# A feed-forward norm taken by halves, one copy of the feed-forward for either kind of weights, and a new order of calls on four engines

## What is computed

```python
# layer 0
h = layernorm(x) * (1 + ca) + sa
x = x + ga * attention(h)        # 16 heads of 16, causal, norm of q and k
h = layernorm(x) * (1 + cb) + sb
x = x + gb * ffn(h)              # silu(h W1) * (h W2), gelu(. H1), gelu(. H2), . W3
# layer 1
h = layernorm(x) * (1 + ca) + sa
x = x + ga * scan(h)             # in-projection, 16-state selective scan over time, gate, out-projection
h = layernorm(x) * (1 + cb) + sb
x = x + gb * (mx_quantize(h) @ mx_quantize(w).T + bias)
```

## Time and profile before

| | |
|---|---|
| median of 3 runs | 4168.96 us (4165.49 to 4177.01) |
| profiled execution | 4167.61 us |
| its span, first to last instruction | 4165.8 us |
| busy | TensorE 85%, VectorE 80%, GpSimd 65%, ScalarE 62% |
| granted TensorE clock, mean | 0.932 of full speed |
| instructions | 50421 |
| read from and written to HBM | 212.25 and 31.46 MB |

### The profile page before, as it was taken

How to read it: one execution, slowest core, us unless ns; L and a number is a source line. 1 busy time by engine, 2 the same in 40 slices (tenths; PEclk the granted TensorE clock), 3 DMA queues, 4 the chain that set the end, 5 groups by cost and what they waited for, 6 DMA issues and landing times. The chain is left out here.

```text
span 4165.8 us, 50421 instructions
## 1 busy us (share of the span) xinstructions
PE 3523.9 (85%) x16621; PEld 2034.0 (49%) x16621; DVE 3318.2 (80%) x3646; ACT 2583.4 (62%) x3703; POOL 2716.0 (65%) x1960
## 2 busy tenths in 40 slices
PE   5687888989899998989898898989999898989513
PEld 3263645546373645546373554636364554636201
DVE  4514878989798888979797887979898897979694
ACT  2345566767667676766666676767667676666431
POOL 0132866768595876768595776759586776768563
PEclk9799999999999999999999999999999999999756
DMA  4630201102030301103030211203030211203000
GB/s 164 258 105 15 97 21 62 62 26 97 6 117 1 97 26 61 62 21 102 6 102 17 82 41 46 77 8 115 1 107 16 76 46 41 82 6 102 0 5 5
DMA packets 69435, 247.81 MB, mean 59 GB/s; under 512 B 9472, under 2 KB 10112, under 8 KB 68736
## 3 DMA queue, kind: packets, MB, share of 16 engines
q1 hardware_dynamic: 66816, 235.35, 16.8%
q10 hardware_dynamic: 2304, 8.39, 0.5%
HBM read 212.25 MB, written 31.46 MB: 59 GB/s over the span
## 5 line engine op out<-in xcount | busy, mean ns | idle before, releaser
L671 POOL TENSOR_TENSOR kept<-kept,hb 128x512 f32<-128x512 f32 x640 | 811.0, 1300 | 71.1 <-DVE hb L1925 70.9
L1916 DVE TENSOR_TENSOR_SCAN hb<-ps,hb 128x512 f32<-128x512 f32 x640 | 745.0, 1205 | 17.5 <-ACT ps L1362 12.7
L929 PE MATMUL ps<-hid_bhi,wring 128*128 128x512 f32 x1536 | 628.0, 409 | 70.9 <-issue 53.6
L929 PE MATMUL ps<-hid_blo,wring 128*128 128x512 f32 x1536 | 619.8, 404 | 0.0
L1362 ACT ACTIVATE ps<-kept,a_neg 128x512 f32<-128x512 f32 x640 | 423.0, 690 | 174.4 <-DVE hb L1916 174.4
L929 PE MATMUL ps<-hid_ahi,wring 128*128 128x512 f32 x1280 | 516.7, 404 | 8.0 <-POOL hid_alo L686 8.0
L639 POOL TENSOR_TENSOR kept<-kept,hb 128x1024 f32<-128x1024 f32 x128 | 300.2, 2360 | 336.3 <-DVE hb L1860 297.7
L929 PE MATMUL ps<-hid_alo,wring 128*128 128x512 f32 x1280 | 505.0, 395 | 0.0
L632 POOL TENSOR_SCALAR_AFFINE_SELECT room<-room 128x512 f32<-128x512 f32 x256 | 217.7, 862 | 427.2 <-ACT room L1569 427.2
L1988 DVE TENSOR_REDUCE room<-ps 128x4 f32<-128x2048 f32 (+3 forms) x256 | 375.2, 1486 | 123.6 <-PE ps L1105 111.3
L1925 DVE TENSOR_TENSOR hb<-hb,ps 128x512 f32<-128x512 f32 x640 | 404.0, 673 | 0.1
(11 more groups left out here) (198 smaller groups left out, 7359.2 us busy)
## 6 DMA issues: line engine op xcount, KB each, us to landing
wring<-w_hi SPq DMA_DIRECT2D x352, 512.0 KB, 3.3
kept<-in_wffn SPq DMA_DIRECT2D x22, 512.0 KB, 6.3
w_hi<-wring SPq DMA_DIRECT2D x22, 512.0 KB, 7.0
w_lo<-wrest SPq DMA_DIRECT2D x22, 512.0 KB, 5.2
xn<-in_x_fm SPq DMA_DIRECT2D x17, 512.0 KB, 3.3
out_fm<-xc ACTq DMA_DIRECT2D x16, 512.0 KB, 5.4
room<-in_wmod SPq DMA_DIRECT2D x2, 1536.0 KB, 8.1
win<-in_win SPq DMA_DIRECT2D x1, 1024.0 KB, 8.4
```

The costliest lines, as they stand in the source:

```text
L671: pool.tensor_tensor(acc[:, m, :], acc[:, m, :], hb[:, s % 8, :], ALU.add).then_inc(acc_done, 1)
L929: mm = pe.matmul(bank(bk), wring[:, r % 3, at + k * P:at + (k + 1) * P], src[i][:, k, :], start=(k == 0 and i == 0), stop=(k == K - 1 and ...
L1916: dve.tensor_tensor_scan(hb[:, s % 8, :], bank(2 + m % 2), hb[:, s % 8, :], 0.0, ALU.mult, ALU.add).then_inc(scanned, 1)
```

## The change

1. The feed-forward's norm has semaphores of its own and goes by halves: mean, centring, square, variance and scaling are two calls each. The affine calls are now `ffn_round(c)` and `ffn_full(c)`, in the order round 0, full 0, round 1, full 1. `att_proj` goes by output half.
2. The first two products of the feed-forward are split: `up_high(1)` and `up_high(0)` need only the rounded halves of h, `up_low(0)` and `up_low(1)` the rests.
3. The weights' rest is no longer stored. The first pass subtracts in place in the stage buffer and measures it, and the buffer is reloaded only after that. If there is a rest, the whole weights are loaded as they are and multiplied in plain float32, in a second copy of the feed-forward. The flag is asked for once in a pass, by TensorE and by SyncE.
4. The order of calls on TensorE, ScalarE, VectorE and GpSimd is new.

The diff, cut to its core:

```diff
-        wrest = sb("wrest", [P, 2, HM * P], F32R)
+        wraw = sb("wraw", [P, 2, HM * P])
 def split_sync(sp):
-            for t in range(FT + 2):
+            for t in range(FT + 1):
                 if t < FT:
                     if t >= 3:
-                        sp.wait_ge(w_split, t - 2)
+                        sp.wait_ge(w_measured, t - 2)
                     sp.dma_start(stage[:, t % 3, :], a["wffn"][t]).then_inc(stage_loaded[t % 3], 16)
...
-                    sp.wait_ge(w_split, r + 1)
-                    sp.dma_start(w_lo[r], wrest[:, r % 2, :].bitcast(F32)).then_inc(lo_stored[r % 2], 16)
...
-                dve.tensor_tensor(wrest[:, t % 2, :], stage[:, t % 3, :], wring[:, t % 3, :].bitcast(F32), ALU.subtract).then_inc(w_split, 1)
+                dve.tensor_tensor(stage[:, t % 3, :], stage[:, t % 3, :], wring[:, t % 3, :].bitcast(F32), ALU.subtract).then_inc(w_split, 1)
 # TensorE: norm, first products, choice
+            def ffn_mean(c):
+                    pe.wait_ge(att_added, since(att_added, c + 1 if att else DC))
+                    mm = pe.matmul(bank(4), mean_mat[:, :], xa[:, c, :], start=(c == 0), stop=(c == DC - 1))
+            def ffn_var(c):
+                    pe.wait_ge(f_cent, since(f_cent, DC))
+                    pe.wait_ge(f_sq, since(f_sq, c + 1))
+                    mm = pe.matmul(bank(4), mean_mat[:, :], ln_s[:, c, :], start=(c == 0), stop=(c == DC - 1))
+            def up_high(n, exact):
+                    pe.wait_ge(h_rounded, since(h_rounded, DC))
+                    wait_tile(0, exact)
+                    if n == 0:
+                        ... tail_y, head_y
+                    else:
+                        ... ff_added, dt_min
+                    up_product(n, 0, exact)
+            def up_low(n, exact):
+                    pe.wait_ge(h_split, since(h_split, DC))
+                    up_product(n, 1, exact).then_inc(up_done, 1)
+                with pe.If(has_rest > 0):
+                    feed_forward(False)
+                with pe.Else():
+                    feed_forward(True)
 # TensorE's order around the norm
-            head_spread(1, 1)
-            att_proj(0)
-            values(3, 0) values(3, 1) values(3, 2) row_sums(3)
-            att_proj(1) att_proj(2) att_proj(3)
-            fin_back(0) fin_back(1)
-            ffn_mean() spread(0, 2) ffn_var() fin_ff(0) spread(1, 2) fin_ff(1)
-            up(0) up(1) up(2) spread(0, 3) up(3) ...
+            fin_back(0) head_spread(1, 1)
+            att_proj(0, 0) att_proj(1, 0) values(3, 0) att_proj(0, 1) att_proj(1, 1)
+            values(3, 1) values(3, 2) row_sums(3)
+            att_proj(2, 1) att_proj(2, 0) att_proj(3, 0) att_proj(3, 1)
+            ffn_mean(0) ffn_mean(1) spread(0, 2) fin_back(1) ffn_var(0) ffn_var(1) fin_ff(0) fin_ff(1)
+            up_high(1) spread(1, 2) up_high(0) up_low(0) up_low(1) up(2) spread(0, 3) up(3) ...
 # TensorE's order in the attention stage (one example)
-            scores(3, 0) out_proj(1) scores_turned(2, 0) fin_mean() head_spread(1, 0) scores(3, 1) values(1, 2)
-            fin_var() scores_turned(2, 1) row_sums(1) scores(3, 2)
+            scores(3, 0) out_proj(1) head_spread(1, 0) scores_turned(2, 0) fin_mean() scores(3, 1)
+            fin_var() scores_turned(2, 1) values(1, 1) values(1, 2) scores(3, 2)
 # VectorE
+            tail_in(3, 0) tail_scan(3, 0) tail_out(3, 0) tail_scan(3, 1) tail_out(3, 1)
-            ffn_scale() times_b(2, 0) ff_add(0) scan(2, 0) times_b(2, 1) ff_add(1) times_c(2, 0) gate_up(0)
+            ffn_scale(0) ffn_scale(1) ff_add(0) ff_add(1) times_b(2, 0) scan(2, 0) times_c(2, 0) gate_up(0)
...
-            scan(11, 0) times_c(11, 0) next_scale() scan(11, 1) ffn_add(1) times_c(11, 1)
+            scan(11, 0) next_scale() times_c(11, 0) times_b(11, 1) ffn_add(0) ffn_add(1) scan(11, 1) times_c(11, 1)
 # GpSimd
-            causal_probs(2, 2) causal_probs(3, 0) quant_at(0, 12) causal_probs(3, 1) quant_at(1, 3) causal_probs(3, 2)
+            causal_probs(2, 2) quant_at(0, 3) quant_at(0, 12) causal_probs(3, 0) causal_probs(3, 1) causal_probs(3, 2) quant_at(1, 3)
 # SyncE, once in a pass
-                for r in range(3, FT):
-                    ... load w_hi[r]
-                    with sp.If(has_rest > 0):
-                        ... load w_lo[r]
+                with sp.If(has_rest > 0):
+                    ... load a["wffn"][r], r = 0 to 21, into wraw
+                with sp.Else():
+                    ... load w_hi[r], r = 3 to 21
```

More of the change, by code:

```diff
@@ L838, in pre_var @@
                 if pre:
[L839 removed]
+                    pe.wait_ge(f_norm, since(f_norm, 0))
                     if att:
@@ L912, in next_var, with wait_tile, product @@
                     mm.then_inc(next_var_done, 1)
-            def product(bk, r, at, src, K, fresh=None):
-                for k in range(K):
-                    if k == K - 1:
-                        with pe.If(has_rest > 0):
-                            pe.wait_ge(rest_loaded[r % 2], since(rest_loaded[r % 2], 16 * (r // 2 + 1)))
-                            for i in range(K):
-                                if fresh is not None:
-                                    pe.wait_ge(hid_split, since(hid_split, fresh + i + 1))
-                                for part_of in src:
-                                    pe.matmul(bank(bk), wrest[:, r % 2, at + i * P:at + (i + 1) * P], part_of[:, i, :],
-                                              start=False, stop=False)
+            def wait_tile(r, exact):
+                if exact:
+                    pe.wait_ge(w_loaded[r % 3], since(w_loaded[r % 3], 16 * (r // 3 + 1)))
+                else:
+                    pe.wait_ge(raw_loaded[r % 2], since(raw_loaded[r % 2], 16 * (r // 2 + 1)))
+            def product(bk, r, at, src, K, exact, fresh=None):
+                for k in range(K):
                     if fresh is not None:
@@ L1160, in att_proj @@
                     pe.wait_ge(o_normed, since(o_normed, quad + 1))
-                    for m in range(DC):
-                        mm = pe.matmul(bank(m), wu[:, quad, m * P:(m + 1) * P], o_sb[:, quad, :], start=(quad == 0), stop=(quad == QUADS - 1))
-                        if quad == QUADS - 1:
-                            mm.then_inc(att_out, 1)
+                    mm = pe.matmul(bank(m), wu[:, quad, m * P:(m + 1) * P], o_sb[:, quad, :], start=(quad == 0), stop=(quad == QUADS - 1))
+                    if quad == QUADS - 1:
+                        mm.then_inc(att_out, 1)
             project(0)
@@ L1309, in tensor_pass, with feed_forward @@
-            spread(1, 11)
-            mid(17)
+            def feed_forward(exact):
+                up_high(1, exact)
+                spread(1, 2)
+                up_high(0, exact)
+                up_low(0, exact)
+                up_low(1, exact)
+                up(2, exact)
+                spread(0, 3)
+                up(3, exact)
+                up(4, exact)
+                up(5, exact)
+                up(6, exact)
+                up(7, exact)
+                spread(1, 3)
+                spread(0, 4)
+                mid(0, exact)
+                mid(1, exact)
+                spread(0, 5)
+                spread(1, 4)
+                mid(2, exact)
+                mid(3, exact)
+                mid(4, exact)
+                spread(0, 6)
+                spread(1, 5)
+                mid(5, exact)
+                mid(6, exact)
+                spread(0, 7)
+                spread(1, 6)
+                mid(7, exact)
+                mid(8, exact)
+                spread(1, 7)
+                spread(0, 8)
+                mid(9, exact)
+                mid(10, exact)
+                spread(0, 9)
+                spread(1, 8)
+                mid(11, exact)
+                mid(12, exact)
+                mid(13, exact)
+                spread(0, 10)
+                spread(1, 9)
+                mid(14, exact)
+                mid(15, exact)
+                spread(0, 11)
+                next_mean()
+                spread(1, 10)
+                mid(16, exact)
+                next_var()
+                spread(1, 11)
+                mid(17, exact)
```

510 lines of the change are left out of this document (247 added, 263 removed).

## The result

The changed kernel took 4176.12 us, median of 12 runs (4168.27 to 4185.08), beside 4165.84 for the kernel before on the same chips (4163.98 to 4177.01). The ratio is 1.0021, with a 95% interval of 1.0014 to 1.0029: a hair slower, and inside the 0.3% that I called no change. I had forecast 4074. The profiled execution took 4173.6 us (span 4171.9).

What follows compares the result with a forecast made beforehand. TensorE, VectorE and GpSimd fill the third stage; TensorE idles 20.4 us a pass in the first two. 14 x (-4.5 - 1) = -77, the rest -18, together -95: 4167.6 to 4072.6, plus 1.4 for the median: 4074; range 4015 to 4140.

Steps and rivals of the forecast that it cites:

- The norm: Ahead of the feed-forward: halves and early high products bring the first gate 4.6 us sooner; -4.5 us a pass, bounds -3, -6.
- The stretch behind the gate: Feed-forward beside the scan's body: TensorE keeps its lead, every spread is met, the tightest with 1.3 us to spare.
- The order in the first stage: Loop's attention stage: TensorE's new order moves work into waits; -1 us a pass, bounds -5 and +3.
- my walk: Call-by-call estimate of the attention stage's new order: its projection ends at 1605.0 for 1605.4.
- a first stage longer than 129 us: Named sign of being wrong: the loop's attention stage, 126.3 us before, takes over 129 us.
- My slower case: After the far jump TensorE fetches each following packet only when it reaches it: 4224 us; chance 0.06.
- The first pass: Weights' split without the stored rest: 1.0 MB a tile for 1.5, 60 us for 90; -12 us, between -17 and -3.
- under 80: Sign to look for in the first pass: the split's stretch, 90 us before, should take under 80.
- The jump: TensorE's one jump a pass over the second feed-forward copy: cost 0, at most 3.3 us; rival exposed, 4124 us, chance 0.14.
- The clock: TensorE's slow stretch in the attention stage: some 4 us of slow clock, counted among what the new order could win.

Runs made afterwards that it cites:

- stage_old: Changed kernel with the old order of calls up to the second attention addition on four engines (but for fin_back(1)): 4103.93 us, 0.9844 of the kernel before.
- first_old: Changed kernel with the old order of calls in the first pass's attention stage alone: 4150.58 us, 0.9966 of the kernel before.
- only_dve_new: Changed kernel where, behind the first pass, VectorE alone keeps the changed order up to the second addition and three engines have the old: 4260.09 us, one run.
- halves_alone: Changed kernel's code (norm by halves, early rounded halves, new split, one choice) with the old order on every engine throughout: 4142.30 us, 0.9945 of the kernel before.
- stage_old_att: Changed kernel with the old order up to the second addition in passes with attention, the changed order in the two closing passes: 4099.66 us, 0.9851 of before.
- tails_paired: Changed kernel, first pass in the old order, with VectorE's tail_out(1, 0), (2, 0), (3, 0) behind their step's second scan as before: 4147.27 us, one run.

## Why the prediction was wrong, by its steps

**The norm: right.** It said 4.6 us to the first gate, and 4.45 came. The first hidden layer was to start 4.5 to 5 us sooner; it starts 26.82 us after the second addition, for 31.97: 5.15. The low products come 11.3 us after the addition, for 10.9 forecast; of this 0.4 us GpSimd's head addition accounts for up to 0.2 (L638 ended at 1880.30, the subtraction's first input was ready at 1880.06). The stretch behind the gate kept the lead and added 1.5 us in a steady pass: -5.9 in all, at the far end of my -3 to -6.

**The order in the first stage: the step that failed.** I took -1 a pass, with bounds of -5 and +3, "by my walk". It was +56.2 us over 14 passes, 4.0 each, and +14.1 in pass 1, so outside the bound. The order itself is 42.0 of the 56.2, by stage_old, which is 3.0 a pass and at the bound's edge; the other 14.2 came into this stage from the rest of the change, for which the sum had no term. The walk followed the end of the stage, on TensorE, with durations of before. It looked at none of the places where calls of VectorE now stand ahead of a maximum. stage_old shows the size of the error: with the order of this stage undone in every pass, the first too, the time is 4103.93 us, inside my range. I had named this as what would be wrong, "a first stage longer than 129 us", but given no rival for it. My slower case was the far jump, and that isn't what happened.

**The first pass: the step failed in sign.** I costed the split by its bytes: 90 us at 344 GB/s, hence -12. In the changed kernel the DMA share falls from 0.68 to 0.45 and the stage is 21.7 us longer, so bytes didn't set it. From the first subtraction to the last measuring it took 107 us (82.0 to 189.2), where I wanted under 80 and it was 92 before. The store is worth 2 to 6 us; the order of calls cost 26 (158.7 to 132.7 in first_old), 11.6 of them by the splits' places, at a granted clock of 0.69 for 0.74.

**The jump: right, nearly.** I took 0 and got about 5 us in the loop. By the Trainium skill (Runtime: NRT & Kernel Launch, Instruction fetch mechanics) a branch outside the pages in hand stalls until the page is there; the trace fits this in two passes of 14, though the gap stands behind the first high product and not ahead of it. That other work covers the jump in the twelve others is argued, not shown.

**The clock: a term that I had left out.** The earlier trace rows told me that the attention stage has a slow stretch, and I counted it only as a possible gain. It is 4.2 us between the two passes shown, and in the changed kernel it is gone; had it stayed, that kernel would have lost more. A longer stage alone doesn't free the clock: pass 7 of only_dve_new takes 139.96 us at 0.91.

**Still open** is which calls of the changed order make its attention stage 6.9 us longer at full clock. That it is the order is shown; that TensorE waits for VectorE's maxima there is read from the waits; but none of the parts put back shortened the stage. Open, too, is why it is 1.0 us a pass longer than before in stage_old, and 30.5 us in all longer than in halves_alone.

## What to carry to other kernels

An order of calls for several in-order engines is one object. Don't cost it by its idle time and its work: walk every call that now stands ahead of a link of the longest chain, on each engine, the half-idle ones too, and give the case that the order loses a chance of its own. Where a change brings a better algorithm and a new order together, measure the two apart; here the norm and what follows it gained 5.3 us a pass, and the attention stage lost 4.0, 3.0 of them by its own new order. The version to use is stage_old_att or stage_old, 1.5% faster than the kernel before.

## What the runs showed of the hardware

The same calls at nearly the same times got a full clock in one pass and not in another: before, at 868.3 to 888.3 us, TensorE was busy for 13.65 of 20 us and the granted clock was 1.00; in the steady passes the granted clock fell in that part of the stage, to 0.71. I can't say what decides it.

GpSimd and VectorE were slower beside each other. Beside a scan (L1897) GpSimd's addition took 4.22 us, where 2.36 is usual, and a scan beside GpSimd's next product took 3.58 for 2.28:

```profile
1777.74 4.22 POOL L629 TENSOR_TENSOR kept<-kept,hb 128x1024 f32<-128x1024 f32 x1 [5.50 <-issue]
```

```profile
1777.53 2.28 DVE L1897 TENSOR_TENSOR_SCAN hb<-hb 128x1024 f32<-128x1024 f32 x1
...
1785.97 3.58 DVE L1897 TENSOR_TENSOR_SCAN hb<-hb 128x1024 f32<-128x1024 f32 x1
```

The Trainium skill (GPSIMD Engine Reference, Specifications) says that the two share their SBUF interfaces and contend when a VectorE instruction has two SBUF inputs; the trace agrees for the scan, whose two inputs both lie in SBUF. In tails_paired that addition took 2.37 us and the stage kept its length; the stretched scans were still there (3.90 and 3.66 us, for 3.58 and 3.11 in the changed kernel), so what they cost is not shown.
